# One stage for projections and attention, its order given by patterns, and the PSUM banks of the scores, sums and maxima divided anew

## What is computed

```python
q = (x @ wq.T).reshape(b, t, NUM_HEADS, 2, HEAD_DIM)       # 16 heads, 2 halves, 16 channels
k = (x @ wk.T).reshape(b, t, NUM_HEADS, 2, HEAD_DIM)
v = (x @ wv.T).reshape(b, t, NUM_HEADS, 2 * HEAD_DIM)
attn1 = _attn(q1, k1, v)                                    # softmax(q1 k1 / 4) v
attn2 = _attn(q2, k2, v)
attn = attn1 - lambda_full * attn2
rms = jax.lax.rsqrt(jnp.mean(attn * attn, axis=-1, keepdims=True) + EPS)
attn = attn * rms * subln_w
return (attn * (1.0 - LAMBDA_INIT)).reshape(...) @ wo.T
```

## Time and profile before

| what | us |
|---|---|
| median of 3 runs | 2691.18 |
| lowest, highest | 2689.74, 2695.02 |
| the profiled execution, its own time | 2691.85 |
| its span | 2690.1 |
| mean granted clock of PE | 0.962 of full speed |

### The profile page before, as it was taken

How to read it: one execution, slowest core, us unless ns; L and a number is a source line. 1 busy time by engine, 2 the same in 40 slices (tenths; PEclk the granted TensorE clock), 3 DMA queues, 4 the chain that set the end, 5 groups by cost and what they waited for, 6 DMA issues and landing times. The chain is left out here.

```text
span 2690.1 us, 41760 instructions
## 1 busy us (share of the span) xinstructions
PE 2448.0 (91%) x15600; PEld 1255.6 (47%) x15600; DVE 1707.7 (63%) x3976; ACT 1206.9 (45%) x1571; POOL 188.6 (7%) x341
## 2 busy tenths in 40 slices
PE   7958999999999999879999999877799999999886
PEld 5832222222222222357888888766233333333365
DVE  2146888888888888483444444432677777777586
ACT  2205666666666666552122222331355555555553
POOL 3000000000000000000000000000111111111103
PEclk9968999999999999899999999988799999999998
DMA  5373311113211100001000000015322212210001
GB/s 190 131 125 96 43 25 25 25 25 40 33 25 25 25 2 1 29 9 40 24 24 23 23 23 24 0 57 138 58 30 38 32 24 37 37 20 2 25 1 63
DMA packets 56645, 108.91 MB, mean 40 GB/s; under 512 B 11808, under 2 KB 22048, under 8 KB 56464
## 3 DMA queue, kind: packets, MB, share of 16 engines
q1 hardware_dynamic: 53936, 96.79, 18.3%
q0 software_dynamic: 2528, 9.70, 1.0%
HBM read 73.75 MB, written 31.46 MB: 39 GB/s over the span
## 5 line engine op out<-in xcount | busy, mean ns | idle before, releaser
L551 ACT ACTIVATE l_prob<-l_p_score 128x1024 f32<-128x1024 f32 (+2 forms) x896 | 827.9, 932 | 699.6 <-PE l_p_score L488 699.6
L583 DVE TENSOR_REDUCE l_maxima<-l_p_ring 128x1 f32<-128x512 f32 x1280 | 823.8, 685 | 232.2 <-PE l_p_ring L465 228.5
L508 PE MATMUL l_p_out<-l_prob,v_all 128*32 128x512 f32 (+3 forms) x3584 | 869.5, 561 | 10.1 <-ACT l_sums L542 6.1
L508 PE MATMUL l_p_out<-l_prob,l_ones 128*32 128x512 f32 (+3 forms) x3584 | 869.5, 561 | 0.0
L488 PEld LDWEIGHTS l_p_score<-xT_l_q,xT_l_k 50*128 50x128 f32 x1792 | 167.6, 184 | 645.7 <-ACT l_prob L551 487.1
L465 PE MATMUL l_p_ring<-xT_l_k,xT_l_q 48*128 48x512 f32 (+3 forms) x1792 | 363.7, 402 | 102.9 <-DVE l_maxima L580 54.0
L488 PE MATMUL l_p_score<-xT_l_q,xT_l_k 50*128 50x512 f32 (+3 forms) x1792 | 428.3, 475 | 13.5 <-DMA xT_l_q<-l_shift_rows 12.0
L580 DVE CUSTOM_DVE_ANT_0 l_masked_scores<-l_p_ring,mask 128x128 bf16<-128x128 f32 (+3 forms) x512 | 232.0, 488 | 117.6 <-PE l_p_ring L465 108.0
L508 PEld LDWEIGHTS l_p_out<-l_prob,v_all 128*32 128x32 f32 x3584 | 135.6, 108 | 275.1 <-issue 219.4
L465 PEld LDWEIGHTS l_p_ring<-xT_l_k,xT_l_q 48*128 48x128 f32 x1792 | 174.9, 192 | 148.2 <-DVE l_maxima L580 77.4
L1042 DVE SCALAR_TENSOR_TENSOR ffn_h<-ffn_p_u,ffn_group_scales,ffn_silu 128x512 f32<-128x512 f32 x64 | 48.0, 751 | 212.0 <-PE ffn_p_u L197 206.2
(11 more groups left out here) (141 smaller groups left out, 2761.4 us busy)
## 6 DMA issues: line engine op xcount, KB each, us to landing
xT_l_q<-q_parts SPq DMA_DIRECT2D x192, 128.0 KB, 5.5
q_parts<-l_part SPq DMA_DIRECT2D x64, 256.0 KB
xT_l_k<-k_parts SPq DMA_DIRECT2D x96, 128.0 KB, 7.6
k_parts<-l_part SPq DMA_DIRECT2D x40, 256.0 KB
xT_l_k<-k_parts SPq DMA_DIRECT2D x96, 64.0 KB, 4.9
x<-in_x_T SPq DMA_DIRECT2D x4, 1024.0 KB, 11.2
xT_l_q<-l_shift_rows SPq DMA_DIRECT2D x256, 4.0 KB
x<-in_L_attn_x POOLq DMA_DIRECT2D x1, 4096.0 KB, 16.0
```

The costliest lines, as they stand in the source:

```text
L508: summing = pe.matmul(p_out[r0:r0 + VD, off:CH], lhs, prob[step % PRING][:, sub, off:CH], start=first, stop=final)
L551: act.activation(prob[step % PRING][:, :, off:CH], p_score[:, step % 2, :, off:CH], ACT.Exp, scale=HD ** -0.5).then_inc(exped, 1)
L583: dve.tensor_reduce(to, scores, AX.X, ALU.max).then_inc(freed, 1)
```

## The change

`qkv_phase` becomes a part of `attention_phase`, so that one list per layer has units, values, pairs, shifts, scores, sums and turns. `projections()` lists the units and values in the old order and sets the first 24 (layer 0) or 20 (layer 1) P among them, from item 28 or 22 on, spread evenly, and X0. `heads()` goes through a fixed string once per head. The q and k buffers now lie where x's columns of the same sequence lay (`xT`), so load(0) and load(1) wait for the values of sequence 0 (V7) and load(2) and load(3) for all values. SP goes through the list: stores, then at V7 loads, then stores again.

PSUM's eight banks are `p_work`, 4 banks, and `p_ring`, now 4. The projections use all four of `p_work`; in the heads three of them are score banks, one for each half of a step in turn, and one is `p_out`. So a step has two exponentials of 512 columns, each with its own wait, and each matmul of S waits for one bank and signals by itself. `copied_after` (1, 1) puts ACT's copy of the sums behind the exponential of the step that follows the chunk's last one. The prob buffers, `sums` and `half` lie where the weights lay, the maxima have two buffers, and the mask is made in layer 1's stage. The lines of the items are now P L438, X L446, S L465, W L484, T L493, exponential L561, copy L551, store L352, loads L317 and L321, ones L335.

```diff
-RING = 3
+RING = 4
...
+WORK_BANKS = 4
+SCORE_BANKS = 3
+PART_BUFFERS = 3
+LOAD_SLOTS = 4
...
+    def projections(self):
...
+        MT = self.q_tiles + self.k_tiles
+        work = []
+        for c in range(NCH):
+            work += [("unit", c * MT + m) for m in range(MT)] + [("values", c * QPC + t) for t in range(QPC)]
+        out, at, shift_at = [], 0, None
+        start = QC * (MT + QPC) + LOAD_SLOTS
+        for i, item in enumerate(work):
+            out.append(item)
+            if shift_at == i:
+                out.append(("shift", 0))
+            while i >= start and at * (len(work) - start) < self.first_pairs * (i + 1 - start):
+                out.append(("pair", *divmod(at, len(self.pairs))))
+                at += 1
+                if at == len(self.pairs):
+                    shift_at = i + 1
...
+    def heads(self):
...
+        while scores < SUM_LAG:
+            out.append(("score", *divmod(scores, S)))
+            scores += 1
+        for _ in range(HEADS):
+            for what in self.pattern:
+                if what == "S" and scores < HEADS * S:
+                    out.append(("score", *divmod(scores, S)))
+                    scores += 1
...
-L0 = Layer("l0", D, D, False, 0.35)
-L1 = Layer("l1", D // 4, D // 4, True, 0.45)
+L0 = Layer("l0", D, D, False, "PPWSWSPPWSPWPSWPSWPSPWSWSPXTSWPSWWSPTSWPSWSPPWSPWWS",
+           24, (1, 1))
+L1 = Layer("l1", D // 4, D // 4, True, "PSWSPPSWWWSPTSWSPXTSWSPWPSPWPSWWPSPWWPS", 20, (1, 1))
...
-        p_score = ps("p_score", [P, 2, 2, CH], F32)
-        p_ring = ps("p_ring", [P, RING, CH], F32)
-        p_out = ps("p_out", [P, CH], F32)
...
+        p_work = ps("p_work", [P, WORK_BANKS, CH], F32)
+        p_score = p_work[:, 0:SCORE_BANKS, :]
+        p_out = p_work[:, SCORE_BANKS, :]
+        p_ring = ps("p_ring", [P, RING, CH], F32)
...
+                else:
+                    sp.wait_ge(v_done, NT // B * (i // 2 + 1))
...
+            for what, *at in L.items:
+                if what == "unit":
+                    store(*at)
+                    if L.shift_store == at[0]:
+                        shift_row(0)
+                elif what == "values" and at[0] == NT // B - 1:
+                    wait_stored(QC * MT)
+                    load(0)
+                    sp.wait_ge(ready, 3)
+                    load_ones(0)
+                    load(1)
+                    load_ones(1)
+                elif what == "score":
+                    break
...
+            wait_stored(L.units)
+            for i in range(2, PAIR_BUFFERS):
+                load(i)
+                load_ones(i)
+            for n in range(1, HEADS):
                 shift_row(n)
...
                 if n == 0 and s == 0:
+
+                    pe.wait_ge(part_lo, L.units)
+                    pe.wait_ge(v_kept, NT)
                     pe.wait_ge(ones_in, 16 * PAIR_BUFFERS * 2 * KH)
...
-                if step >= 2:
-                    pe.wait_ge(exped, step - 1)
                 for sub in range(2):
+                    part = 2 * step + sub
+                    if part >= SCORE_BANKS:
+                        pe.wait_ge(exped, part - SCORE_BANKS + 1)
...
-                act.activation(prob[step % PRING][:, :, off:CH], p_score[:, step % 2, :, off:CH], ACT.Exp,
-                               scale=HD ** -0.5).then_inc(exped, 1)
-
-            for step in range(SUM_LAG):
+                for sub in range(2):
+                    part = 2 * step + sub
+                    act.wait_ge(scored, part + 1)
+                    act.activation(prob[step % PRING][:, sub, off:CH], p_score[:, part % SCORE_BANKS, off:CH], ACT.Exp,
+                                   scale=HD ** -0.5).then_inc(exped, 1)
...
+            copies = {}
+            for n in range(HEADS):
+                for qc, s in enumerate(L.qc_last):
+                    copies.setdefault(min(n * S + s + L.copied_after[qc], HEADS * S - 1), []).append((n, qc))
+            for step in range(HEADS * S):
                 exp(*divmod(step, S))
...
+                for at in copies.get(step, []):
+                    copy_out(*at)
```

More of the change, by code:

```diff
@@ L90, in __init__ @@
         self.qc_last = [max(s for s, x in enumerate(self.steps) if x[0] == qc) for qc in range(QC)]
-        self.lead = lead
-        self.items = self.order()
+        self.pattern, self.first_pairs, self.copied_after = pattern, first_pairs, copied_after
+        self.items = self.projections() + self.heads()
+        later = [x[1] for x in self.items[self.items.index(("shift", 0)):] if x[0] == "unit"]
+        self.shift_store = later[1] if len(later) > 1 else None
+        work = [x for x in self.items if x[0] in ("unit", "values")]
+        self.work_at = {x: i % WORK_BANKS for i, x in enumerate(work)}
+        self.work_ahead = {x: work[i - WORK_BANKS] if i >= WORK_BANKS else None for i, x in enumerate(work)}
         self.filled_at, self.bank_at = {}, {}
@@ new lines, in attention_phase @@
+        ones_rows = attn_area.taken_by(f"{L.name}_ones_rows", [2, T], F32R, NT * D - T)
+        ones = sb("ones", [P, VD], F32)
+        maxima = sb("maxima", [P, 2, 2 * KT, 2], F32)
+        shift = sb("shift", [P, 2 * KT], F32)
+        shift_rows = [sb(f"shift_rows{i}", [2 * KT, P], F32R) for i in range(2)]
+        if L.causal:
+            masked_scores = [sb(f"masked_scores{i}", [P, CH], BF16) for i in range(2)]
+            mask, mask_made = sb("mask", [P, CH], F32), sem("mask_made")
+        recip = sb("recip", [P, QPC, 2], F32)
@@ L369, in attention_phase @@
+        stored = [sem(f"stored{r}") for r in range(PART_BUFFERS)]
         q_in = [sem(f"q_in{i}") for i in range(PAIR_BUFFERS)]
```

366 lines of the change are left out of this document (160 added, 206 removed).

## The result

The changed kernel takes 2734.49 us (median of 4 runs, 2728.0 to 2737.21) where before takes 2693.1 (4 runs, 2689.74 to 2700.61): the ratio of the means is 1.0146, 95% interval 1.0118 to 1.0175. It is slower, by 41 us; forecast were 16 us less. 2734 also lies above the range (2632 to 2714).

The account below looks back on a forecast made before the run. PE was taken to bound layer 0's heads, PE with some waits layer 1's, loads the leads. Terms 14 − 40 + 3 + 5 − 1.4 + 1 gave −18 us, about 2673, stated as 2675; range 2632 to 2714.

Parts of the forecast that it names:

- the copy stall: In each head ACT's copy of chunk 0's sums waits for T, delaying the exponential, S and W: 1.28 us lost.
- a low clock behind gaps of 15 us: In the projections, PE's wait for stores leaves the granted clock low afterwards: 2.8 us in each layer.
- Layer 0's heads, +14: PE's items fall from 27.99 to 27.64 us, the copy's wait adds 1.28: 28.9 per head, +14 us over 31.
- Layer 1's heads, −40: Fewer runs and bank waits, less two stalls: 18.47 us per head against 19.78, −40 us over 30.5 heads.
- the second stall of 0.75: In layer 1's heads the second half of S9.2 waits for the exponential behind chunk 1's copy: +0.75 us.
- The fourth bank, 1.9 (2.3 with the other waits): In layer 1's heads four maxima banks remove two waits of P, 1.9 us, and 0.4 of other waits.
- Projections and leads, +3 and +5: Loads ahead of stores stall PE and 24 or 20 P move in: first S 3 and 5 us later.
- The two waits for the stores: In the projections PE stands while stores queue behind loads: 16.3 us in layer 0, 14.2 in layer 1.
- The term for the 24 P: In layer 0's projections 24 P between the units cost 0.46 us each, 11 us in all.
- Exponentials of 512, nothing: ACT's 1,792 half exponentials hide under PE's 1.66 us step, costing nothing but the copy's stall.
- the halves of S come apart: Rival, chance 0.16: wait and increment of every single S matmul cost 0.04 to 0.05 us each, 2710 to 2720.
- The rival on the copy stall: Chance 0.08: wait for T delays both exponentials of step 9, steps run bunched, 2 us not 1.28: about 2715.

Follow-up runs that it names:

- e9: The changed kernel with the copy of chunk 0's sums one exponential later and three banks for the maxima instead of four: 2886.93 us, 1.072 of before.
- e1: The changed kernel with ACT's copy of chunk 0's sums one exponential later (`copied_after` 2 for chunk 0): 2649.35 us, 0.9839 of before.
- e2: The changed kernel with T of the head before put ahead of the last W of chunk 0: 2647.73 us, 0.9837 of before.
- e6: The changed kernel with the first matmul of S8.10 (layer 1: S8.6) done five times, filling the wait: 2699.14 us, 1.0019 of before.
- e3: The kernel before in its own order, with three single score banks, four banks for maxima and exponentials of 512: 2721.98 us, 1.012 of before.
- e4: The changed kernel with only load(0) sent at V7, other loads after all stores, their ones awaited at head 2: 2682.43 us, 0.9966 of before.
- e7: The kernel before in its own order, with three single score banks, exponentials of 512 and three banks for maxima: 2819.01 us, 1.048 of before.

## Why the prediction was wrong

**The step that failed** is the price of the copy stall, "1.28 us lost in each head". The stall is there, in every head, and takes 1.30 us; W starts 2.31 us after T (650.72 to 653.03) where 2.30 was summed. What it sets off stood in the sum at nothing: PE's array is idle for 0.81 us, and behind 16 such gaps in layer 0 the granted clock is 0.5 for about 3.4 us, at 1.54 us each. In layer 1 it costs 0.5 us per head. Together these are 40 of the 63 us by which the spans missed the sum. I had priced a low clock behind gaps of 15 us and looked at none that short; the trace of before has a granted clock of 1.00 in both layers' heads although layer 1 had gaps of 0.67 and 0.88 us in each head. So the rows of before would not have told it, but a rival that prices it was missing. The length of one gap doesn't decide it: in the change itself the same gap lowers the clock in one head and not in another, and in e9 five gaps of 0.56 to 0.79 us per head of layer 0 never do.

By the terms of the sum:

- *Layer 0's heads, +14.* An undisturbed head has 29.12 (forecast 28.92), which is 6 us more over 31 heads; the falls of the clock are 25. Together 45. e1, e2 and e6 show both parts apart.
- *Layer 1's heads, −40.* An undisturbed head has 18.83 (forecast 18.47): −29. The falls give back 15, which leaves −14 of the −14.9 measured. That 18.47 is near 18.83 is luck, for two terms were wrong and nearly cancel: the second stall of 0.75 is in no head, and what is left beside the stall of 1.30 is 17.5 where PE's items were summed to 16.44. Before, 17.9 are left of the head beside the 1.9 of the two waits for maxima. So the new order saved about 0.4 us of items and small waits, where 1.4 was summed (1.0 for fewer runs, 0.4 for other waits).
- *The fourth bank, 1.9 (2.3 with the other waits).* Under the new patterns it is worth 2.3 us in layer 1, and 4.7 in layer 0 (e9), where I had nothing. That it costs a bank of scores, and that the old order would pay for that (e3), I had not seen.
- *Projections and leads, +3 and +5.* 6.7 and 8.1. The two waits for the stores were hit to 0.3 us, and e4 shows that the order on SP's queue is their cause. The end of layer 0's projections came 3.7 us later than summed (217.02 − 28.81 = 188.2 against 184.5). The term for the 24 P was too small: a P between two units adds 0.66 us and not 0.46 (the two rows behind this list: 3.38 from P to P with one unit of 2.72 between), a second P behind it 0.34, and 20 × 0.66 + 4 × 0.34 = 14.6 where 11 was summed.
- *Exponentials of 512, nothing.* Right in layer 0's heads with the old order: in e7, which there has only the split, the head is 28.46 as before. The rival "the halves of S come apart" gave 2710 to 2720, but its mechanism, a cost of every single S, is out with that. By the rule of the Trainium skill ("TensorE: Matmul & The Clock Gate", Part 3, on the semaphore tail) 16 more signals in a head would be an estimated 16 × 26.3 ns = 0.42 us; e7 shows no such cost. That the work behind S hides the signals is my guess and not shown.
- *The rival on the copy stall* (0.08, 2715) had the right place and a cost per head of 2 us in place of 1.28; the mean measured is 1.30 + 0.8 = 2.1 in layer 0 and 1.30 + 0.5 = 1.8 in layer 1. That its number fits is luck: its reason, bunched steps, was not the one.

PE's timeline in layer 0's projections:

```profile
129.25 0.50 PE L438 MATMUL l_p_ring<-xT_all 48*128 48x512 f32 x2
...
132.63 0.50 PE L438 MATMUL l_p_ring<-xT_all 48*128 48x512 f32 x2
```

The stall itself was right in place and size, and moving the copy by one exponential turns the change into a gain of 1.6%. So the slower time is no property of the merged stage or of the bank division under these patterns: the one number `copied_after` turns it round by itself, and SP's order takes another 52 us (e4).

What stays open is why the clock falls behind some stalls and not behind others. The pattern in time is regular (in layer 0 six fast heads, then three slow and two fast in turn; in layer 1 one fall in three heads), and the gap is the same in all. No run varied the length of the gap alone, or its place, and none tells why the five gaps of a head in e9 lower nothing. That the idle time is needed for the falls is shown (e6), that it is enough is not. Open too is what the new order would do with the old banks, for the patterns were run with three score banks only.
